# Split operands for the output products of a 16-head attention, three scan states instead of eight

## What is computed

```python
# l1_ffn: a ternary FFN with a Hadamard transform between its products
gate, up = bitlinear(x, w_gate), bitlinear(x, w_up)
return h_bitlinear(silu(gate) * up, w_down)

# l2_xattn: 16 heads of 128
q, k, v = rmsnorm(x @ Wq, gq), rmsnorm(ctx @ Wk, gk), ctx @ Wv
attn = softmax(einsum('bqhd,bkhd->bhqk', q, k) * 128 ** -0.5)
out = einsum('bhqk,bkhd->bqhd', attn, v).reshape(B, S, 2048)
return out @ Wo

# l3_xattn: a selective scan with 16 states per channel, on ctx alone
state = state * exp(dt * A) + (dt * u) * b
y = einsum('bdn,bn->bd', state, c)
```

## Time and profile before

| | us |
|---|---|
| median of 3 runs | 3502.61 |
| lowest and highest run | 3500.46, 3504.72 |
| the profiled execution | 3490.28 |
| span of the profiled execution, first to last instruction | 3488.6 |

### The profile page before, as it was taken

The page is one execution under the profiler, slowest core; times in us unless marked ns, Lnnn a source line. Parts: engine busy times, 40 slices in busy tenths (PEclk is TensorE's granted clock), DMA queues, the critical chain, the costliest instruction groups (busy, mean ns, idle before and its releaser), DMA issues. The chain is left out here.

```text
span 3488.6 us, 42689 instructions
## 1 busy us (share of the span) xinstructions
PE 3122.0 (89%) x14213; PEld 1833.0 (53%) x14244; DVE 2621.1 (75%) x3478; ACT 1844.0 (53%) x3430; POOL 1443.2 (41%) x957
## 2 busy tenths in 40 slices
PE   7869797999997888799999999999999787998985
PEld 3437554333334555455555555555555366786663
DVE  7855689877774888468888888887788864765886
ACT  5644343666663655565666666666656432664220
POOL 1122279000000000067777777777778654223430
PEclk9879899999998999899999999999999898999998
DMA  4137735222216400245555555455454346675421
GB/s 133 40 118 277 277 103 151 58 58 58 64 32 150 63 1 1 85 153 155 182 170 167 162 189 168 154 169 180 159 171 144 127 182 211 249 254 192 145 73 60
DMA packets 229749, 478.66 MB, mean 137 GB/s; under 512 B 36239, under 2 KB 69647, under 8 KB 213664
## 3 DMA queue, kind: packets, MB, share of 16 engines
q1 hardware_dynamic: 223296, 459.19, 41.2%
q0 software_dynamic: 6240, 16.81, 1.3%
HBM read 387.51 MB, written 92.06 MB: 137 GB/s over the span
## 5 line engine op out<-in xcount | busy, mean ns | idle before, releaser
L2393 POOL TENSOR_TENSOR l2x_inflow<-l2x_dtu,l2x_rows_b 128x512 f32<-128x512 f32 x256 | 437.2, 1708 | 254.8 <-DVE l2x_state L2279 253.5
L178 POOL TENSOR_TENSOR ln_work<-ln_work,minus_half 128x4 f32<-128x4 f32 (+1 forms) x34 | 33.1, 975 | 1000.4 <-DVE ln_work L166 1000.3
L2279 DVE TENSOR_TENSOR_SCAN l2x_state<-l2x_decay,l2x_inflow 128x512 f32<-128x512 f32 x256 | 403.9, 1578 | 0.0
L2409 POOL TENSOR_TENSOR l2x_y_sum<-l2x_y_sum,l2x_state 128x512 f32<-128x512 f32 x224 | 387.0, 1728 | 29.2 <-DVE l2x_state L2288 29.2
L1324 DVE TENSOR_REDUCE l1x_mx<-psum 128x2 f32<-128x1024 f32 x256 | 308.4, 1219 | 96.6 <-PE psum L1166 95.2
L1281 ACT ACTIVATE l1x_split<-psum 128x1024 f32<-128x1024 f32 x256 | 262.0, 1025 | 155.6 <-PE psum L1166 155.6
L2288 DVE TENSOR_TENSOR l2x_state<-l2x_state,l2x_rows_c 128x512 f32<-128x512 f32 x256 | 298.2, 1165 | 7.1
L2151 ACT ACTIVATE l2x_decay<-l2x_dt,a_neg 128x512 f32<-128x512 f32 x256 | 181.6, 721 | 165.5 <-DVE l2x_state L2279 165.1
L126 PE MATMUL psum<-l2x_probs_t,l2x_v_tok 128*128 128x512 f32 x512 | 236.3, 605 | 16.1 <-ACT l2x_qt L212 12.9
L126 PE MATMUL psum<-l2x_xt,l2x_wq 128*128 128x512 f32 x512 | 231.9, 597 | 8.6 <-issue 8.6
L2086 ACT ACTIVATE l2x_probs<-psum,l2x_soft,l2x_norms 128x512 f32<-128x512 f32 x256 | 195.6, 774 | 79.9 <-DVE l2x_soft L2218 79.9
(11 more groups left out here) (459 smaller groups left out, 7147.5 us busy)
## 6 DMA issues: line engine op xcount, KB each, us to landing
l2x_rows_b<-l3x_xd_dram SPq DMA_DIRECT2D x256, 256.0 KB, 3.9
l2x_rows_c<-l3x_xd_dram SPq DMA_DIRECT2D x256, 256.0 KB, 3.5
l2w_raw<-l_w SPq DMA_DIRECT2D x38, 1024.0 KB, 6.7
l2x_wkv<-l2x_kv_dram SPq DMA_DIRECT2D x32, 1024.0 KB, 6.8
l2w_raw<-l_w SPq DMA_DIRECT2D x38, 512.0 KB, 4.7
l1x_heads_dram<-l1x_stage SPq DMA_DIRECT2D x32, 512.0 KB, 3.3
l2x_wq<-l_wq SPq DMA_DIRECT2D x16, 1024.0 KB, 5.1
l2x_wo<-l_wo SPq DMA_DIRECT2D x16, 1024.0 KB, 7.3
```

The source lines that it names most:

```text
L2279: dve.tensor_tensor_scan(state[:, s % KEPT, :], decay[:, s % 3, :], inflow[:, s % 3, :], 0.0, ALU.mult, ALU.add).then_inc(scan_done, 1)
L2393: pool.tensor_tensor(inflow[:, s % 3, :], dtu[:], rows_b[:, s % 3, :], ALU.mult).then_inc(inflow_ready, 1)
L2409: pool.tensor_tensor(total, total, state[:, s % KEPT, :], ALU.add).then_inc(added, 1)
```

## The change

It has three parts. **Weights**: in the FFN phase eight blocks of `l2_wo` are loaded (512 KB each, behind the clearing write in SP's program), ACT copies each to float32r (`output_high`, at odd steps, behind the SiLUs), GpSimd subtracts that from the raw block (`output_low`), and SP writes both parts to `wo_dram`, which the attention phase loads from, 2 MB a unit instead of 1. SP's program waits for the eight writes at its end. **Results**: DVE's `value` now writes the scaled result into `inv_b`, ACT copies it to the high part of `ot` (`high`), DVE writes the difference to the low part (`low`), and the output products become split products, which wait for the fourth `low` of the unit. **Buffers**: `KEPT` goes from 8 to 3, `y_sum` and `inv_b` to one buffer, and the squares of the keys go to a part of `q_sq`.

```diff
@@ l1_ffn, SP, behind the clearing write
+            def output_weight(p):
+                sp.dma_start(o_raw[:, p % 2], a["l2_wo"][p * 2 * P:(p + 1) * 2 * P, :].rearrange("(c p) n -> p c n", p=P)).then_inc(o_in[p % 2], 16)
+            def output_parts(p):
+                m, half = divmod(p, 2)
+                sp.wait_ge(o_lo, p + 1)
+                sp.dma_start(g["wo_dram"][m, :, :, 2 * half:2 * half + 2, :], o_parts[:].bitcast(F32)).then_inc(o_stored, 16)
+            output_weight(0)
+            output_weight(1)
+            for p in range(2 * G2):
+                output_parts(p)
+                if p + 2 < 2 * G2:
+                    output_weight(p + 2)
             sp.wait_ge(emptied, 16)
+            sp.wait_ge(o_stored, 2 * G2 * 16)
@@ l1_ffn, ACT
+            def output_high(p):
+                act.wait_ge(o_in[p % 2], (p // 2 + 1) * 16)
+                if p:
+                    act.wait_ge(o_stored, p * 16)
+                act.activation(o_parts[:, 0], o_raw[:, p % 2], ACT.Copy).then_inc(o_hi, 1)
...
                     gate(t)
+                if t % 2 and t // 2 < 2 * G2:
+                    output_high(t // 2)
                 if 0 <= t - 3 < T1:
                     y_turned(t - 3)
@@ l1_ffn, POOL
+            def output_low(p):
+                pool.wait_ge(o_hi, p + 1)
+                pool.tensor_tensor(o_parts[:, 1], o_raw[:, p % 2], o_parts[:, 0].bitcast(F32), ALU.subtract
+                                   ).then_inc(o_lo, 1)
             for b in range(NB):
                 ln.pool(pool, b)
+                output_low(2 * b)
+                output_low(2 * b + 1)
@@ l2_xattn
-KEPT = 8
+KEPT = 3
...
-        ot, inv_b = sb("ot", [P, 4, S]), sb("inv_b", [P, 2, S])
+        ot, inv_b = sb("ot", [P, 2, 4, S], F32R), sb("inv_b", [P, S])
...
-        y_sum = sb("y_sum", [P, 2, S])
+        y_sum = sb("y_sum", [P, S])
@@ l2_xattn, PE, output
                     pe.wait_ge(wo_in, (u + 1) * 16)
+                    pe.wait_ge(ot_lo, (u + 1) * 4)
                     for t in tiles:
-                        ring.wait_for(pe, 0, free=f"out{u}_{t}", drained=[f"pv{u}_3"])
-                        ring.fill(product(pe, bank(f"out{u}_{t}"), [(ot[:, h, t * P:(t + 1) * P], wo[:, h, :])
-                                                                    for h in range(4)]))
+                        ring.wait_for(pe, 0, free=f"out{u}_{t}")
+                        ring.fill(split_product(pe, bank(f"out{u}_{t}"), [
+                            ([ot[:, k, h, t * P:(t + 1) * P] for k in range(2)], [wo[:, k, h, :] for k in range(2)])
+                            for h in range(4)]))
@@ l2_xattn, ACT
-                    if u or h >= 2:
-                        before = f"pv{u}_{h - 2}" if h >= 2 else f"pv{u - 1}_{h + 2}"
-                        ring.wait_for(act, 0, drained=[before])
-                    copy(act, "act", ring, f"iv{u}_{h}", inv_b[:, h % 2, :], bank(f"iv{u}_{h}"))
+                    since(act, ot_lo, u * 4 + h)
+                    copy(act, "act", ring, f"iv{u}_{h}", inv_b[:], bank(f"iv{u}_{h}"))
+            def high(u, h):
+                if u >= 0:
+                    ring.wait_for(act, 0, drained=[f"pv{u}_{h}"])
+                    act.activation(ot[:, 0, h, :], inv_b[:], ACT.Copy).then_inc(ot_hi, 1)
...
                 turn(u, 1)
+                high(u, 0)
                 decays(u, 5)
...
                 query(u + 1, 2)
+                high(u, 1)
                 decays(u, 6)
...
                 turn(u, 3)
+                high(u, 2)
                 decays(u, 9)
                 key_scale(u + 1, 3)
                 inverse(u, 3)
+                high(u, 3)
                 context(u + 1, "v", v_tok)
@@ l2_xattn, DVE
-                    ring.drain(dve.tensor_tensor(ot[:, h, :], bank(f"pv{u}_{h}"), inv_b[:, h % 2, :], ALU.mult),
-                               f"pv{u}_{h}")
+                    ring.drain(dve.tensor_tensor(inv_b[:], bank(f"pv{u}_{h}"), inv_b[:], ALU.mult), f"pv{u}_{h}")
+            def low(u, h):
+                if u >= 0:
+                    dve.wait_ge(ot_hi, u * 4 + h + 1)
+                    dve.tensor_tensor(ot[:, 1, h, :], inv_b[:], ot[:, 0, h, :].bitcast(F32), ALU.subtract).then_inc(ot_lo, 1)
...
                 gather(u, 4)
+                low(u, 0)
                 maxima(u, 2)
...
                 gather(u, 7)
+                low(u, 1)
                 maxima(u, 3)
...
                 scan(u, 9)
+                low(u, 2)
                 gather(u, 9)
                 value(u, 3)
                 scan(u, 10)
+                low(u, 3)
                 gather(u, 10)
@@ l2_xattn, POOL, add_state
                 if n == 1:
-                    since(pool, y_read, u - 1)
+                    since(pool, y_read, u)
```

More of the change, by code:

```diff
@@ L1489, in l1_ffn @@
         top = sb("top", [P, 1])
+        o_raw, o_parts = sb("o_raw", [P, 2, 2, D]), sb("o_parts", [P, 2, 2, D], F32R)
         order = []
@@ L1513, in l1_ffn @@
         empty_made, emptied, top_made = sem("empty_made"), sem("emptied"), sem("top_made")
+        o_hi, o_lo, o_stored = sem("o_hi"), sem("o_lo"), sem("o_stored")
+        o_in = [sem(f"o_in{k}") for k in range(2)]
         ln = LayerNorm(g, sem)
@@ L1840, in l2_xattn @@
         sem, sb = ph.sem, ph.sb
-        wq, wo = [sb(n, [P, DC, D]) for n in ("wq", "wo")]
+        wq, wo = sb("wq", [P, DC, D]), sb("wo", [P, 2, DC, D], F32R)
         wkv = sb("wkv", [P, 2, CC, D], F32R)
@@ L1845, in l2_xattn @@
         k_tok, v_tok = sb("k_tok", [P, ST, D]), sb("v_tok", [P, ST, D])
-        k_sq, q_sq = sb("k_sq", [P, S]), sb("q_sq", [P, 4, S])
+        q_sq = sb("q_sq", [P, 4, S])
         qt, kt = sb("qt", [P, 4, S]), sb("kt", [P, 4, S])
@@ L1870, in l2_xattn @@
         b_in, c_in = [[sem(f"{n}_in{k}") for k in range(3)] for n in "bc"]
+        ot_hi, ot_lo = sem("ot_hi"), sem("ot_lo")
         ln = LayerNorm(g, sem)
@@ L1883, in _, with query_weight, output_weight @@
         def _(sp):
-            def weight(w, name, u, arrived, rows=False):
+            def query_weight(u):
                 cols = slice((u % G2) * D, (u % G2 + 1) * D)
-                src = a[name][cols, :] if rows else a[name][:, cols]
-                sp.dma_start(w[:], src.rearrange("(c p) n -> p c n", p=P)).then_inc(arrived, 16)
+                sp.dma_start(wq[:], a["l2_wq"][:, cols].rearrange("(c p) n -> p c n", p=P)).then_inc(wq_in, 16)
+            def output_weight(u):
+                sp.dma_start(wo[:].rearrange("p h c n -> p (h c n)").bitcast(F32),
+                             g["wo_dram"][u % G2].rearrange("p h c n -> p (h c n)")).then_inc(wo_in, 16)
             def context(b):
@@ L1928, in _ @@
             key_weight(0)
-            weight(wq, "l2_wq", 0, wq_in)
+            query_weight(0)
             for k, n in enumerate(("l2_gq", "l2_gk")):
@@ L1937, in _ @@
             value_weight(0)
-            weight(wo, "l2_wo", 0, wo_in, rows=True)
+            output_weight(0)
             ring.wait_filled(sp, 0, "q0_3")
-            weight(wq, "l2_wq", 1, wq_in)
+            query_weight(1)
             ring.wait_filled(sp, 0, f"v0_{ST - 1}")
@@ L1946, in _ @@
                         ring.wait_filled(sp, 0, f"out{u - 1}_{ST - 1}")
-                        weight(wo, "l2_wo", u, wo_in, rows=True)
+                        output_weight(u)
                     if n == 5 and u >= 1:
@@ L1957, in _ @@
                         ring.wait_filled(sp, 0, f"q{u + 1}_3")
-                        weight(wq, "l2_wq", u + 2, wq_in)
+                        query_weight(u + 2)
                     row_b(u * NS + n + 2)
@@ L2111, in context @@
                                 cols = slice(h * P, (h + 1) * P)
-                                act.activation(k_sq[:, cols], bank(f"k{u}_{t}")[:, cols], ACT.Square,
+                                act.activation(q_sq[:, 3, cols], bank(f"k{u}_{t}")[:, cols], ACT.Square,
                                                accum_out=norms[:, u % 2, 2, h, t:t + 1]).then_inc(k_squared, 1)
@@ L2293, in skip_term @@
                     tile = u_in[:, u % 2, :]
-                    dve.scalar_tensor_tensor(tile, tile, g["skip"][:, u % G2:u % G2 + 1], y_sum[:, u % 2, :], ALU.mult,
+                    dve.scalar_tensor_tensor(tile, tile, g["skip"][:, u % G2:u % G2 + 1], y_sum[:], ALU.mult,
                                              ALU.add).then_inc(y_read, 1)
@@ L2400, in add_state @@
                 s = u * NS + n
-                total = y_sum[:, u % 2, :]
+                total = y_sum[:]
                 pool.wait_ge(gathered, s + 1)
                 if n == 1:
-                    since(pool, y_read, u - 1)
+                    since(pool, y_read, u)
                     pool.tensor_tensor(total, state[:, (s - 1) % KEPT, :], state[:, s % KEPT, :], ALU.add
@@ L3747, in program @@
             "kv_dram": nc.dram_tensor("l2x_kv_dram", [3, 4, P, 2 * CC * S], F32).ap(),
+            "wo_dram": nc.dram_tensor("l2x_wo_dram", [G2, P, 2, DC, D], F32).ap(),
```

## The result

The changed kernel took 3601.61 us (median of 4 runs, 3598.71 to 3609.44) where the kernel before took 3501.53 us beside it (4 runs, 3495.48 to 3504.72): 1.0291 times as long, 95% interval 1.0269 to 1.0314. The forecast was 3594 us, with a range of 3552 to 3626. The profiled execution took 3604.02 us, its span is 3602.2.

What follows compares the result with a forecast made beforehand. FFN was taken as bound by PE and VectorE handing tiles to each other, attention by PE. 71 + 3 + 17 = +91 us took the profiled 3490.28 to 3581; the runs' median, 12.3 higher, gave 3594, range 3552 to 3626.

Steps and rivals of the forecast that it cites:

- The stall: FFN stage: first raw-weight load lands behind the clearing write, so ScalarE, VectorE and PE stand; +71 us, bounds 58 to 80.
- The first rival: FFN stage: the first load lands at once, not waiting for the clearing write; 3523 us in all, chance 7%.
- The other copies: FFN stage: seven more ScalarE copies of 1.0 us, partly covered by its waiting, 0.4 each; +3 us, bounds 0 and 7.
- Attention: Attention-and-scan stage: PE's saving on output products against VectorE's added `low` work; +17 us, ends -8 and +41.
- The ten plain units: Attention: PE waits 1.6 us and saves 1.33 a unit, so +0.25 each, +2.5 us together.
- the output group: Attention, PE: 48 split products at 0.25 us take 12.0 us instead of 13.33, saving 1.33 us a unit.
- `low(0)` and `low(1)`: Attention, VectorE: subtractions right behind gathers 4 and 7, taken as 1.5 us each, ends 0.69 and 1.58.
- The four units behind a layernorm: Attention: slack only 0.58 us and VectorE already late, so PE's saving is lost; +2.4 us each, +9.6 together.
- The wait at the squares product: Attention: two `low` push head 3's query copy by 3.0 us past 1.4 us of slack; PE waits 1.6 us.
- `low(2)`, `low(3)`, `high`, `ot_lo`: Attention: two `low` in VectorE's waits, `high` under ScalarE's idle time, output's wait for `ot_lo` before PE arrives; all cost nothing.
- Three states, single buffers, larger `wo`: Attention: fewer kept states, one `y_sum` and the 2 MB `wo` load delay nothing; `wo` bounded at 1 us a unit.
- Rival 2: Attention: load also lands at once, VectorE's idle time swallows all four `low`, PE keeps its saving; 3485 us, chance 4%.

Runs made afterwards that it cites:

- Experiment 4: Changed kernel with the raw-weight loads and stores of the parts issued on GpSimd's queue instead of SP's: 3534.44 us, ratio 1.0105 to the kernel before.
- 2: Changed kernel with the eight ScalarE copies at FFN tiles 8 to 15, GpSimd's subtractions moved to match: 3517.21 us, ratio 1.0058 to the kernel before.
- experiment 10: Changed kernel, copies at tiles 6-8, 10-12, 14, 15; scan 7, gather 7, `low(1)` behind head 3's biases; GpSimd waits in router's stage: 3472.72 us, ratio 0.9928.
- Experiments 5: Changed kernel with copies at tiles 8 to 15, and scan 7, gather 7 and `low(1)` moved behind head 3's biases on VectorE: 3479.24 us, ratio 0.9941.
- 6: Changed kernel with copies at tiles 8 to 15, and `low(1)` alone moved behind head 3's biases on VectorE: 3480.75 us, ratio 0.9950.
- experiment 1: Changed kernel with the first two raw-weight loads issued ahead of the clearing write on SP's queue: 3566.91 us, ratio 1.0206 to the kernel before.

## Why the prediction was right

- **The stall** (+71 forecast): 69.0 us at VectorE's first addition, where 69.6 was worked out. Each link held: the load came with the end of the write, the wait stood on ScalarE ahead of the halves, and VectorE and PE stood behind. Experiment 4 shows the reason, the place behind the write on SP's queue, and 2 the size: 72 us go with the wait. The first rival had the load land at once; it fell. One step is finer than I had it: I let SP issue the load at once and the load wait its turn, but SP took 71.6 us to issue it, until 1158.2. How late a load would be that is issued at once and only stands behind the write, no run shows.
- **The other copies** (+3): 6.3 us for eight in experiments 2 and 10, 0.8 each, where I had 0.4. I had counted ScalarE's 0.62 us of waiting ahead of `yt` as cover. It covers only about a quarter of a microsecond of each copy. The first copy lies within the 69.0 us; seven more at 0.8 make 74.6 of the 78.2. The remaining 3.6 (1.5 forecast, for the clock) were not traced further.
- **Attention** (+17): 18.3, but its parts differ. The ten plain units were to lose 0.25 us each; six took 78.8 us, a gain of 0.75, and four 80.2 to 80.4, a loss of 0.7. Two terms were mis-sized: the output group takes 11.28 us, not 12.0 (0.235 a product, not 0.25), and `low(0)` and `low(1)` take 1.75 us, not 1.5, as the row of gathers had them only nearly. One was missing: PE's clock behind the wait, 1.4 to 1.6 us in four of these units and in two of those behind a layernorm, some 9 us in all, half of what the stage lost. The four units behind a layernorm lost 4.2, 3.8, 2.6 and 2.6 us (forecast 2.4), the first two with the slow clock; the last unit lost 7.7 (3.4): VectorE starts it 2.6 us later than in before, and four `low`, at 1.19, 1.75 and twice 0.67, make 4.3. The first unit gained 1.3 where I had a loss of 1.6: I had it without an output group, but one ends it too. That the sum came out so near is partly luck.
- **The wait at the squares product** was named, and it is there in all 15 units, mostly above the 1.6 us forecast (2.3 on average).
- **`low(2)`, `low(3)`, `high`, `ot_lo`**: nothing, as forecast. The two `low` take 0.67 us each, and PE never stands before the output group for `ot_lo`. GpSimd's subtractions in the FFN stage were to cost nothing too: they did slow VectorE's normalizing (2.45 us for 0.55 at three tiles of the change), and experiment 10, where they meet none, is no shorter for it than 2.
- **Three states, single buffers, larger `wo`**: nothing, as forecast, the first by its own run. The single buffers have none; in the changed kernel GpSimd waits 0.7 us a unit for the one `y_sum` (about 0.6 forecast), and ScalarE 2.9 us in all for the one `inv_b`.
- **The router's stage** was not in the sum. Its 9 us come and go in the kernels here, with and without the change.

Rival 2 named the place where the change decides, the slack ahead of the squares product, and took a gain for possible only with `low` under 0.7 us. Experiments 5 and 6 reach it with `low` as dear as it is, by moving it.

## What to carry to other kernels

Before a new load goes behind existing DMAs, add up the bytes ahead of it on the same queue and look up which engine stands still until it lands; a later place in the program or another queue is enough. When work is added to an engine that isn't the bound, look not at its share but at the stretch where it has no gap and at who waits at the end of it: a subtraction of 1.75 us moved past one such end was worth 37 us. And when a stage that was not touched changes by a few microseconds, look at it in every trace at hand before giving it a cause.

## What the runs showed of the hardware beyond that

SP itself stood still: the first two small loads behind the clearing write took 75.07 us to issue, the first store in experiment 1 37.26, where such an issue takes 0.6 otherwise. The loads of the change (count, then shortest, middle and longest time to issue, in ns):

```profile
L1537 SPq DMA_DIRECT2D l1f_o_raw<-l_wo x8: 611/612/71609, 1086.6 to 1406.0; - x8
```

SP issues in order, so whatever it had to issue next would have been late too. A wait of PE of 2.5 us was followed by a granted clock of 0.62 in some units and 1.00 in others; what decides between them stays open. And what `low`, which reads and writes SBUF, takes on VectorE goes by what GpSimd does when it begins. The two instructions of GpSimd beside the second and third `low` of unit 12 (at 2598.13 and 2613.88 above), then its subtraction beside VectorE's first additions:

```profile
2597.61 1.73 POOL L2448 TENSOR_TENSOR l2x_inflow<-l2x_dtu,l2x_rows_b 128x512 f32<-128x512 f32 x1
...
2614.04 1.63 POOL L2448 TENSOR_TENSOR l2x_inflow<-l2x_dtu,l2x_rows_b 128x512 f32<-128x512 f32 x1 [6.24 <-DVE l2x_state L2330]
```

```profile
1190.01 2.36 POOL L1814 TENSOR_TENSOR l1f_o_parts<-l1f_o_raw,l1f_o_parts 128x1024 fp32r<-128x1024 f32 x1 [69.98 <-ACT l1f_o_parts L1679]
```

In all 32 `low` of the first two heads an inflow of GpSimd is already under way, and they take 1.67 to 1.76 us, but for one of 1.19; in all 32 of the last two it begins 0.15 to 0.17 us behind `low`, which takes 0.67. The additions of the FFN stage, which read PSUM, kept their 0.69 us although GpSimd's subtraction had begun.
